# Layer 1 as one block, an FP4 rounding with one step fewer, and expert lists whose first two rounds hold one expert each

## What is computed

```
scale = max(max(|block|) / 6, 1e-12)
q     = GRID[searchsorted(MID, |x/scale|)] * sign(x/scale) * scale      # GRID 0, .5, 1, 1.5, 2, 3, 4, 6
out   = fp4(silu(fp4(x) @ fp4(wg).T) * (fp4(x) @ fp4(wu).T)) @ fp4(wd).T
```

## Time and profile before

| | us |
|---|---|
| median of three timed runs | 1240.42 |
| the profiled execution | 1234.21 |
| its span, from the first to the last instruction | 1232.3 |
| experts begin, by DVE's first instruction | 670.25 |
| attention 1 begins, by its first DMA | 903.45 |
| feed-forward 1 begins, by its first transpose | 1090.04 |

### The profile page before, as it was taken

One profiled execution on the slowest core, in us unless ns is written; L12 is line 12 of the kernel. 1 busy time (PEld: TensorE's weight loads), 2 busy tenths in 40 slices (PEclk: granted clock), 3 DMA queues, 4 the chain that ended last, 5 costly groups with the idle time before them and its releaser, 6 DMA issues. The chain is left out here.

```text
span 1232.3 us, 25141 instructions
## 1 busy us (share of the span) xinstructions
PE 947.5 (77%) x8604; PEld 648.2 (53%) x8604; DVE 817.7 (66%) x1683; ACT 637.9 (52%) x2132; POOL 433.1 (35%) x332
## 2 busy tenths in 40 slices
PE   6789999998989898996712597678429888867764
PEld 3456556575656575755602464455315555545553
DVE  5777877777786869674656825113125799759996
ACT  2565776868686867674200243122117888843322
POOL 2334432433233333341000578888720233200221
PEclk9899999999999999999556699788758999988878
DMA  7574344434344444531501124347320000000000
GB/s 203 156 189 108 86 119 104 118 89 117 99 117 109 114 106 101 131 93 37 138 3 59 30 72 76 62 59 162 30 75 1 2 1 1 1 1 9 18 18 26
DMA packets 89009, 93.62 MB, mean 76 GB/s; under 512 B 18800, under 2 KB 62304, under 8 KB 88944
## 3 DMA queue, kind: packets, MB, share of 16 engines
q1 hardware_dynamic: 78576, 84.12, 25.9%
q0 software_dynamic: 10368, 8.66, 5.0%
HBM read 24.36 MB, written 10.70 MB: 28 GB/s over the span
## 5 line engine op out<-in xcount | busy, mean ns | idle before, releaser
L843 POOL TENSOR_TENSOR qk_cos<-qk_raw,const 128x512 f32<-128x512 f32 x128 | 181.2, 1417 | 303.2 <-ACT qk_raw L595 303.2
L581 ACT ACTIVATE prob<-psS,neg_max 128x96 f32<-128x96 f32 x512 | 167.9, 342 | 74.2 <-DVE neg_max L676 73.6
L442 PE MATMUL psQ<-a_xnT,weights 128*128 128x512 f32 x250 | 146.2, 669 | 2.7 <-ACT a_xnT L627 2.0
L550 PEld LDWEIGHTS psO<-probT,v_windows 96*64 96x64 f32 x2048 | 71.6, 140 | 133.7 <-ACT probT L655 112.5
L691 DVE TENSOR_TENSOR qk_roped<-qk_cos,qk_swapped 128x512 f32<-128x512 f32 x128 | 122.3, 955 | 0.2
L550 PE MATMUL psO<-probT,v_windows 96*64 96x64 f32 x2048 | 89.5, 231 | 35.4 <-ACT probT L655 35.1
L1505 POOL DMA_INDIRECT ex_rows<-rows,ex_index x64 | 68.5, 1070 | 120.1 <-DMA ex_index<-lists 101.2
L1516 POOL DMA_INDIRECT sums<-ex_y,ex_index x64 | 97.3, 1520 | 24.0 <-issue 18.3
L581 ACT ACTIVATION_READ_ACCUMULATOR prob<-psS,neg_max 128x1 f32 x512 | 105.4, 206 | 0.0
L682 DVE TENSOR_TENSOR qk_swapped<-qk_swapped,const 128x512 f32<-128x512 f32 x128 | 92.7, 724 | 16.2 <-DMA qk_swapped<-qk_raw 15.4
L655 ACT COPY probT<-psT 96x512 f32<-96x512 f32 x128 | 76.8, 600 | 46.7 <-PE psT L530 46.6
(11 more groups left out here) (317 smaller groups left out, 1932.3 us busy)
## 6 DMA issues: line engine op xcount, KB each, us to landing
qk_swapped<-qk_raw SPq DMA_DIRECT2D x512, 64.0 KB, 2.0
v_windows<-v_tok SPq DMA_DIRECT2D x32, 384.0 KB, 4.4
v_windows<-v_tok SPq DMA_DIRECT2D x32, 256.0 KB, 3.7
mod<-mod_rows SPq DMA_DIRECT2D x12, 512.0 KB, 6.7
ex_w<-in_L_ffn_W SPq DMA_DIRECT2D x16, 256.0 KB, 3.2
v_windows<-v_tok SPq DMA_DIRECT2D x32, 96.0 KB, 2.1
rows<-rt_h SPq DMA_DIRECT2D x8, 256.0 KB, 2.4
sums<-rt_zeros SPq DMA_DIRECT2D x8, 256.0 KB, 2.7
```

Source lines behind the costliest of these rows:

```text
L442: last = nc.tensor.matmul(bank, k.wqkvT[:, col:col + P], xnT[:, :], start=True, stop=True)
L550: ins = nc.tensor.matmul(psO[D * j:D * j + D, i * P + a * HALF:i * P + (a + 1) * HALF], vw[:, par, a, t, hd], probT[:, 2 * j + i, a * HALF ...
L581: last = nc.scalar.activation(prob[:, s, 2 * j + i, :], psS[:, s, j, i * KW:(i + 1) * KW], ACT.Exp, bias=nmax[:, s, 2 * j + i:2 * j + i + ...
L843: nc.gpsimd.tensor_tensor(rcos[:, half, :], raw[:, half, :], k.const[:, K_COS:K_COS + T], ALU.mult).then_inc(cos_done, 1)
```

## The change

1. **Lists.** `ROUNDS` replaces `GROUPS` in the loops: expert 0, expert 1, then three rounds with two experts. A one-expert round has half the columns. SP reads the index of expert 0 back after round 0 and that of expert 1 after round 1.
2. **FP4.** The exponent step keeps two bits with `and` and sets others with `or` in the same instruction, and the clamp becomes `max` in the two steps that add and take off MAGIC. The step L1199 is gone; nine remain. The sign is carried by a negative scale. One function serves weights, inputs and hidden values.
3. **Layer 1 as one block.** `phase_layer1` holds attention and feed-forward, without a meeting of the engines between them and with the feed-forward's banks laid over those of attention. All eight inputs are normalised by ACT, modulated by POOL and rounded by `quantise2`: those of sequences 0 to 5 in the loop, 6 behind it, 7 in step with the hidden values of sequence 1. The turn of input 0 and the first gates stand in attention's last sequence.

```diff
+ROUNDS = ((0, 1), (1, 1)) + tuple((e, GROUP) for e in range(GROUP, E0, GROUP))
...
-    done = own.mark(v.tensor_scalar(q.binade.bitcast(U32), q.xn.bitcast(U32), EXPONENT, None, ALU.bitwise_and))
+    done = own.mark(v.tensor_scalar(q.binade.bitcast(U32), q.xn.bitcast(U32), BINADE, RAISE, ALU.bitwise_and, ALU.bitwise_or))
     yield
     dve.wait_ge(own.sem, done)
-    done = own.mark(v.tensor_scalar(q.binade, q.binade, 1.0, None, ALU.max))
-    yield
-    dve.wait_ge(own.sem, done)
-    done = own.mark(v.scalar_tensor_tensor(out=q.total, in0=q.binade, scalar=MAGIC, in1=q.xn, op0=ALU.mult, op1=ALU.add))
+    done = own.mark(v.scalar_tensor_tensor(out=q.total, in0=q.binade, scalar=MAGIC, in1=q.xn, op0=ALU.max, op1=ALU.add))
...
-            for g in range(GROUPS):
+            for g, (e0, n) in enumerate(ROUNDS):
                 sp.wait_ge(ids_ready, g + 1)
...
-                if g == 0:
-                    sp.wait_ge(list_stored, 16)
-                    index_of(0, 0, 0)
-                    index_of(1, 1, 0)
+                if g < 2:
+                    sp.wait_ge(list_stored, 16 * (g + 1))
+                    index_of(g, g, 0)
...
+                    if t == 2 and not next1:
+                        turn_xq(0)
                     apply(b, par, t)
...
-                if not next1:
-                    out_project(b, par)
             turns(body)
+            gate_up(0, range(2))
+            out_project(B - 1, (B - 1) % 2)
+            gate_up(0, range(2, TILES))
+            turn_xq(1)
+            for b in range(B):
+                if b + 1 < B:
+                    gate_up(b + 1, range(TILES))
+                if b + 2 < B:
+                    turn_xq(b + 2)
+                down(b)
...
             def body(b, par, first, next1, next2):
-                steps = quantise2(b - 2) if 0 <= b - 2 < EARLY else iter(())
+                steps = quantise2(b - 2) if b >= 2 else iter(())
...
-                    if u == 5 and 0 <= b - 1 < EARLY:
+                    if u == 5 and not first:
                         finish2(b - 1)
-                    for _ in range((0, 0, 2, 2, 0, 1, 3, 2)[u]):
+                    for _ in range((0, 0, 2, 2, 0, 1, 2, 2)[u]):
...
             turns(body)
+            reciprocals(B - 1)
+            for _ in quantise2(B - 2):
+                pass
+            for _ in residual(B - 1):
+                pass
+            finish2(B - 1)
             for b in range(B):
+                product(b)
+                later = quantise2(B - 1) if b == 1 else iter(())
+                for _ in quantise_hidden(b):
+                    next(later, None)
+                next(later, None)
+                if b > 0:
+                    gate_down(b - 1)
+            gate_down(B - 1)
```

More of the change, by code:

```diff
@@ L1221, in fp4_steps @@
     dve.wait_ge(own.sem, done)
-    done = own.mark(v.tensor_scalar(q.scale, q.amax, 1.0 / 6.0, 1e-12, ALU.mult, ALU.max))
+    done = own.mark(v.tensor_scalar(q.scale, q.amax, -1.0 / 6.0, -1e-12, ALU.mult, ALU.min))
     yield
@@ L1285, in quantise @@
         dve.wait_ge(self.ld, 16 * 7)
-        last, = fp4(self.nc, dve, self.own, [Fp4(self.w[:, :], self.q[:, :], self.WIDTH, self.bufs)])
-        last.then_inc(self.quantised, 1)
+        for _ in fp4_steps(self.nc, dve, self.own, Fp4(self.w[:, :], self.q[:, :], self.WIDTH, self.bufs), self.quantised):
+            pass
     def take(self, dve):
@@ L1802, in copy_oT, with copy_xqT, gates, copy_hqT @@
                 nc.scalar.copy(oT[:, par, t * P:(t + 1) * P], psO[:, 0:P]).then_inc(oT_ready, 1)
+            def copy_xqT(b):
+                act.wait_ge(f_turned, b + 1)
+                wait(act, gated, b * TILES)
+                nc.scalar.copy(xqT[:, :], psQ[:, :]).then_inc(xqT_ready, 1)
+            def gates(b, tiles):
+                wait(act, hq_ready, b - 1)
+                for t in tiles:
+                    act.wait_ge(gated, b * TILES + t + 1)
+                    nc.scalar.activation(silu[:, b % 2, t, :], psG[t % 2][:, 0:F1], ACT.Silu)
+                    nc.scalar.copy(up[:, b % 2, t, :], psU[t % 2][:, 0:F1]).then_inc(gate_out, 1)
+            def copy_hqT(b):
+                for t in range(TILES):
+                    act.wait_ge(h_turned, b * TILES + t + 1)
+                    wait(act, f_ready, b)
+                    nc.scalar.copy(hqT[:, 0:2, t * P:(t + 1) * P],
+                                   psHT[t % 2][:, 0:2 * P].rearrange("p (c q) -> p c q", c=2))
+                    nc.scalar.copy(hqT[0:F1 - 2 * P, 2, t * P:(t + 1) * P],
+                                   psHT[t % 2][0:F1 - 2 * P, 2 * P:3 * P]).then_inc(hqT_ready, 1)
             normalise(0)
@@ L1825, in body @@
                         exps(b, t + 1, 1)
-                    if t == 3 and 0 <= b - 1 < EARLY:
+                    if t == 3 and not first:
                         normalise2(b - 1)
@@ L1834, in body @@
                         copy_hT(b + 2)
-                if not next1:
-                    scale_y(b)
+                    if t == 2 and not next1:
+                        copy_xqT(0)
             turns(body)
+            gates(0, range(2))
+            scale_y(B - 1)
+            gates(0, range(2, TILES))
+            copy_xqT(1)
+            for b in range(B):
+                if b + 1 < B:
+                    gates(b + 1, range(TILES))
+                if b == 0:
+                    normalise2(B - 1)
+                if b + 2 < B:
+                    copy_xqT(b + 2)
+                copy_hqT(b)
         @block.sync
@@ L1861, in body @@
                     norm.root_bias(pool, b + 2)
-                if 0 <= b - 1 < EARLY:
+                if not first:
                     norm2.root_bias(pool, b - 1)
@@ L1866, in _ @@
             turns(body)
+            norm2.root_bias(pool, B - 1)
+            modulate2(B - 1)
+            for b in range(B):
+                pool.wait_ge(f_read, b + 1)
+                nc.gpsimd.tensor_tensor(k.x[:, b, :, :], k.x[:, b, :, :], fmul[:, :, :], ALU.add).then_inc(f_sum, 1)
         @block.vector
@@ L2167, in phase_store @@
-def phase_store(nc, k):
-    with ExitStack() as ctx:
-        block = ctx.enter_context(nc.Block())
-        @block.sync
-        def _(sp):
-            for b in range(B):
-                sp.dma_start(k.out[b].rearrange("(t p) c -> p t c", p=P), k.x[:, b, :, :]).then_inc(k.stored, 16)
-            sp.wait_ge(k.stored, 16 * B)
-STOP = 9
+            reciprocals(B - 1)
+            for _ in quantise2(B - 2):
+                pass
+            for _ in residual(B - 1):
+                pass
+            finish2(B - 1)
```

369 lines of the change are left out of this document (117 added, 252 removed).

## The result

The changed kernel takes 1217.18 us (median of four runs, 1216.96 to 1218.67), the kernel before beside it 1239.01. The ratio is 0.9829, 95% interval 0.9801 to 0.9857: faster by 1.4 to 2.0%, which is 17.7 to 24.7 us. The forecast was 1216.5 with a range of 1208 to 1226, faster with 0.95. The profiled execution took 1216.96.

The account below looks back on a forecast made before the run. DVE was taken to bound the feed-forward and the middle of attention 1, POOL the experts. Gains of 3.9 + 7.4 + 9.1 + 0.2 + 1.4 + 1.9 = 23.9 take the execution from 1234.21 to 1210.3, the median to 1216.5; range 1208 to 1226.

Parts of the forecast that it names:

- junction: Between attention and feed-forward: the first hidden product starts at 1096.9 in place of 1100.75, 3.9 us less.
- hidden step: Feed-forward on DVE: the clamp goes from eight rounds and the fused two-operation step stays at 0.89, 7.4 us less.
- waits: PE in the feed-forward: new waits after slow-clock starts cost 1.0, old ones under input 7 save 1.2; net gain 0.2.
- attention's loop: Attention 1: the clamp, 0.46 with its gap, goes from three sequences in which DVE is full; 1.4 us less.
- the inputs: Feed-forward, inputs 6 and 7: normalising and modulating move off DVE under other rounds, input 7 keeps 2.7; gain 9.1.
- the lists' term: Experts: the first list comes 4.6 earlier, so POOL's first scatter goes from 725.54 to 723.65; gain 1.9.
- the rival of the fused step at half rate: Feed-forward on DVE: the two-operation step runs at half rate, 6.6 us more, 1223; chance 0.06.
- The rival that PE's clock falls at every turn: Feed-forward: PE's round of 13.7 binds in place of DVE's 12.6, 6.6 where the forecast has 1.0, so 1222; chance 0.18.
- The slow rival: PE stays in the low clock for the whole feed-forward, 45 us in all, 1261; chance 0.03.
- a gather costs 2.13: Experts on POOL: price per gather while DVE builds lists, making the 4.6 head start worth 2.2 gathers.
- The line that was to prove the prediction wrong here: Lists: the prediction is wrong if POOL's last scatter comes no earlier.
- The rival of no overlap at the junction: ACT holds the first gates behind input 6's normalisation, so the first product starts no earlier: 1220; chance 0.06.

Follow-up runs that it names:

- ten_steps: The changed kernel with the ten-step rounding of before (exponent bits, clamp at 1, multiplication by MAGIC): 1228.59 us, ratio 0.9939 to the kernel before.
- slot7: The changed kernel with POOL's passes for input 7 held until sequence 1's product and input 7's rounding started four steps later: 1218.87 us, ratio 0.9861.
- psum_iota: The changed kernel with the row of 32 numbers for the one-hot matrices in PSUM as float32, not SBUF as bfloat16: 1214.92 us, ratio 0.9837.
- psum_old_lists: The changed kernel with the lists of before (four rounds of two experts) and the row of 32 numbers in PSUM: 1216.33 us, ratio 0.9818.
- no_overlap: The changed kernel with the turn of input 0 and the gates of sequence 0 behind attention's last projection: 1221.28 us, ratio 0.9851.

## Why the prediction came out right, step by step

The time and the sign are right. Of six terms three hold (junction, hidden step, waits), attention's loop gave about half, the inputs lost a fifth, and the lists' term was lost whole. That the median came within 0.7 of the forecast is partly luck: the profiled pair gives 17.3 (1234.21 to 1216.96) where the sum had 23.9, and the 6.2 that was added to come from that execution to the median is 0.2 in the changed kernel.

- **Junction, 3.9 predicted, 4.8 measured.** Its parts: 0.95 to POOL's start (0.94 predicted), 6.23 to the first rounding step (7.21), 4.79 for the rounding (4.75), 3.51 and 0.78 for residual and finish (3.5 and 0.8). The 7.21 was read where POOL's bias step took 0.67 and its first pass 1.77 beside a working DVE; here DVE is idle, and they take 0.29 and 1.27, which is 0.9 of the 1.0. The cover behind which the gates lie is 5.4 (1092.8 to 1098.2), not 2.8. POOL's first pass in the kernel before:

```profile
1068.28 1.77 POOL L1852 TENSOR_TENSOR a_h<-a_h,mod 128x512 f32<-128x512 f32 x1 [1.82 <-ACT a_h L265]
```

- **One step fewer for the hidden values, 7.4: measured 7.6** by ten_steps, where a plain round is 13.50 against 12.57. The fused step is at 0.89, so the rival of the fused step at half rate is out.
- **Inputs 6 and 7, 9.1: 1.9 less.** Input 7 keeps about the 2.7 in round 1, but its two POOL passes cost round 0 another 1.87. The step that failed is "both go to ACT and POOL under other rounds": I had priced the move at nothing. slot7 shows that the 1.87 goes with the passes. Round 1 from product to product is 15.34, as forecast (15.3).
- **Waits on PE, net 0.2: measured 0.0.** One wait of 1.17 and one hidden by input 7, worth 1.65, which are the slow starts as forecast. The rival that PE's clock falls at every turn is out: three plain rounds in a row (1126.81 to 1164.53) have a granted clock of 1.00 and take 12.57 to 12.58 without a wait; the fourth has 0.73, and the wait follows it. The slow rival, low clock throughout, is out with it. (The lower end of this term should read -5.4, 1.2 less 6.6.)
- **Attention's loop, 1.4: measured 0.8** in the pair, 0.9 by ten_steps. I had taken three sequences in which DVE is full at 0.46 each; DVE is full there, but a sequence takes 19.88 to 20.22 before and 19.79 after. The term's size was wrong because POOL's two passes stand beside other DVE steps now, and those last longer by more. One sequence before, then after:

```profile
1009.30 1.42 DVE L1243 SCALAR_TENSOR_TENSOR a1x_total<-a1x_binade,a1x_total 128x512 f32<-128x512 f32 x1
1010.75 1.64 DVE L1246 TENSOR_TENSOR weights<-a1x_total,a1x_scale 128x512 f32<-128x512 f32 x1
```

```profile
1012.37 1.64 DVE L1206 TENSOR_TENSOR weights<-a1x_total,a1x_scale 128x512 f32<-128x512 f32 x1
1013.93 1.75 DVE L1946 TENSOR_TENSOR a_mul<-weights,mod 128x512 f32<-128x512 f32 x1
```

  Each takes 0.68 or 0.69 by itself, so in this sequence the passes (after: from 1012.13 to 1015.13) cost DVE 1.7 before and 2.0 after, which eats 0.3 of the 0.46. In the next one it is 1.9 and 2.0, in the one ahead 2.0 and 2.0. This is read from rows; no run was made for it.
- **Lists, 1.9: measured -0.1.** The front part came as forecast (store at 5.55, first gather 5.0 earlier). What failed is the step in which a gather costs 2.13, so that 4.6 is worth 2.2 gathers: the mean over eight gathers was carried to a stretch where the next two take 6.46 and 3.06. Behind that stands a second fault: the sum lets POOL stay full from its first gather on. Where the gathers aren't slowed it idles for the last list (8.54 in psum_iota), so a head start is worth nothing there either, as psum_old_lists shows. The line that was to prove the prediction wrong here came true: POOL's last scatter starts 221.93 after the first one-hot matrix, and 221.82 before.
- **Not foreseen:** 2.93 lost ahead of the experts in code that is the same. Lists (2.0), input 7 (1.9), attention (0.6) and waits (0.2) fell short by 4.7; junction and hidden step gave 1.1 more (rounding leaves 0.3). The profiled pair so has 20.0 for the change instead of 23.9; the medians differ by 21.8.

The rival of no overlap at the junction was about rightly priced: 3.9 there, and no_overlap loses 3.5.

## What to carry to other kernels

Ahead of starting one engine earlier, ask what it runs beside: here POOL's gathers beside DVE's two-operand steps took up to seven times as long, and one operand moved to PSUM (as float32) set them free. Follow the early result to its first reader; a list that comes 5 us sooner is worth nothing while that reader waits for the last list. Work that is moved to another engine is free only under steps of the first that don't stop it: on DVE here a reduction, but not the narrow scaling step.

## What was not expected of the hardware

- A gather's issue on POOL takes 0.94 to 0.96 (the first one 1.18) beside DVE instructions with one SBUF operand and up to 6.46 beside the same ones with two. The 6.46 comes again in each of the seven traces that have split rounds with both operands in SBUF.
- A POOL pass of 1.27 holds DVE's steps, here by up to 1.1: a narrow step goes from 0.21 to 1.07, the 1408-wide exponent step from 0.89 to 1.83, though both read one operand; the reduction stays at 1.62. The Trainium skill (the same section of "SBUF — State Buffer") has it that whoever comes first keeps the other out for a whole instruction, which these rows bear out. So does POOL's add of the feed-forward: where it starts 0.16 behind DVE's product (1127.57 against 1127.41) it takes 2.58 and the product 1.62, and in ten_steps, 0.04 ahead of it, 1.26 and 2.71.
- The same code ahead of the experts ended up to 7.4 us apart (671.41 to 678.82) in single executions. That spread is larger than most edits here. The rank matmuls at one clock or the other make 1.4 to 1.6 of it; the cause of the rest is open.
